# Exponentials of two tiles behind one activation-table load in the expert loop of a fused layer

## The chip, the cores and the metric

The kernel runs on one core of a Trainium2 chip. The metric is the device time of one execution in microseconds (us), here the median of three executions. Five engines work side by side, each through a queue of its own in program order: PE (matrix multiply), ACT (activation functions), DVE and POOL (elementwise work), SP (which here issues nearly all transfers). They meet only through semaphores: an instruction that waits holds up everything behind it on its engine.

## The reference, cut to what matters

One transformer layer over B x T = 4 x 768 = 3072 rows of width 192: retention attention, then a layer of small experts. The change touches only the second part, for each row:

```python
z = jnp.einsum('nd,sdr->nsr', xf, P)                 # S = 8 spaces, R = 16
scores = jnp.einsum('nsr,smr->nsm', z, C)            # M = 64 experts in each space
topv, topi = jax.lax.top_k(scores, K)                # K = 4
w = jax.nn.softmax(topv, axis=-1)
h = jax.nn.gelu(jnp.einsum('nsr,nskrh->nskh', z, W1g) + b1g)
yl = jnp.einsum('nskh,nskhr->nskr', h, W2g) + b2g
comb = jnp.einsum('nskr,nsk->nsr', yl, w)            # then two small dense layers
```

The kernel computes all 64 experts of a space and multiplies each by its gate: the softmax weight if it is among the four largest scores, else 0.

## The kernel before

The rows stand in 24 tiles of 128 (`TILES`) and in 6 blocks of 4 tiles (`NBLK`). After the attention comes the expert loop: 192 groups, `g = 8 i + n`, with 24 iterations `i` of 8 groups `n` each. Four iterations work off one block (block `i // 4`), each group four hidden matrices of 128 x 512. Every engine has this loop written out in its own order.

**One group.** PE: `duo_firsts(g+1)`, `tri_first(g+1)` (L700), `second(g-2)` (L755), `duo_gates(g+1)` (L732), `two_first(g+1)` (L700). ACT: the "duo" gelu (L1051, two banks), the "tri" gelu (L1058), the "two" gelu (L1060). DVE: multiplication of duo by its gates (L1491), of two (L1494). POOL: multiplication of tri by its gates `wbc` (L1686). SP: `spread(g+3)` (L323), which loads the gates `wbc` for three groups ahead and waits until group g-1 is through on DVE and POOL. `second(g)` waits for all three products of its group.

**The gates.** In the same loop the gates of tile `i + 5` (`LEAD`) are made, while `i` is at work. For tile t, in iteration i = t - 5 (some of it at the end of the iteration before): `scores` (PE, L560), `copy_scores` (ACT, L927), `largest` and `mark` (DVE, into `mr`), `distances` (POOL, L1574 and L1576, scores minus the largest, into `dist`), at n = 3 `exps` (ACT, L931), `chosen_exps` and `normaliser` (DVE, L1355 to L1349), `weights` (POOL, L1585), at n = 5 `turn_gates` (PE, L566, transposes into bank `PBANK`), at n = 6 `keep_gates` (ACT, L938), at n = 6 and 7 `high_part` and `low_parts` (POOL, L1592 to L1600, the gates in three bf16 parts in the one buffer `wp`). The results go out to memory: `store_rows` (L275, 2 transfers) at n = 7, and `store_gates` (L282, 3 transfers from `wp`) at n = 0 of the next iteration. They come back once all four tiles of a block are stored: `load_gates(i)` (L305, 3 transfers into `wst`, from which `duo_gates` computes) and `spread`.

Exp and gelu stand in different activation tables, so each `exps` at n = 3 has a table load ahead of it and the next gelu has one too.

Three lines order the transfers. `high_part` overwrites `wp` and so waits, on POOL, until what was stored from it has landed; `load_gates` waits, on SP, for all stores of its block:

```python
                if tile > 0:
                    pool.wait_ge(s["w_stored"], 48 * tile)
...
                sp.wait_ge(s["w_stored"], 48 * min(TILES, 4 * blk + 4))
```

`w_stored` rises by 16 when a transfer has landed, 48 for a tile. `duo_gates(8 i)`, which PE has in group 8 i - 1, waits for `wst_ld`, the landing of `load_gates(i)`.

Of the kernel before, what the change touches and what calls it, by code (L numbers as in the profile page):

```python
# [49 lines left out]
def fused_layer(nc, t):  # L50
# [8 lines left out]
    with ExitStack() as ctx:  # L59
# [39 lines left out]
        with ExitStack() as region:  # L99
            x2 = alloc(region, "x2", [P, 4, D])  # L100
            sc = alloc(region, "sc", [P, S, M + 4])
            mr = alloc(region, "mr", [P, S, M + 4])
# [6 lines left out]
            alloc(region, "spare", [P, 888])  # L109
            x2T = alloc(region, "x2T", [P, 2, BLK])  # L110
            wT_even = alloc(region, "wT_even", [P, 4, BLK])
            dist = alloc(region, "dist", [P, S * M + S * TOPK])
# [105 lines left out]
        def gated(a, b):  # L218

            half = a // HALF  # L220
            return (gate_a, gate_b)[half][:, a - half * HALF:b - half * HALF, :, :]

        def place(g):
# [6 lines left out]
        def _(sp):  # L230
# [131 lines left out]
            for g in range(GROUPS):  # L362
                i, n = divmod(g, 8)
                tile = i + LEAD
                if g + 3 < GROUPS:
                    spread(g + 3)
                if n == 1 and i > 0:
                    load_w2(i, 1)
                if n == 2 and i + 1 < NIT and (i + 1) % 4 != 0:
                    load_gates(i + 1)  # L370
                if n == 4 and i + 1 < NIT and (i + 1) % 4 == 0:
                    load_gates(i + 1)
                if n == 3 and i % 2 == 0 and i + 2 < NIT:
                    load_z(i // 2 + 1)
                if n == 5 and i % 4 == 1 and i > 1:
                    store_out(i // 4 - 1)
                if n == 6 and i in (1, 2, 3):
                    store_z(i + 2)
                if n == 6 and i + 1 < NIT:
                    load_w2(i + 1, 0)  # L380
                if n == 7 and tile < TILES:
                    store_rows(tile)
                if n == 0 and LEAD < tile <= TILES:
                    store_gates(tile - 1)
            store_out(NBLK - 1)
            sp.wait_ge(s["stored"], 16 * 2 * NBLK)
# [3 lines left out]
        def _(pe):  # L390
# [392 lines left out]
            for g in range(GROUPS):  # L783
# [13 lines left out]
                if n == 4 and tile + 1 < TILES:  # L797
                    pe.wait_ge(s["wT_done"], tile)
                    if i > 4:
                        pe.wait_ge(s["fin_h"], 2 * ((i - 1) // 4))  # L800
                    scores(tile + 1, PBANK)
# [30 lines left out]
        def _(act):  # L832
# [96 lines left out]
            def exps(tile):  # L929
                act.wait_ge(s["p_dist"], LENT + tile + 1)  # L930
                act.activation(dist[:, :], dist[:, :], ACT.Exp).then_inc(s["e_done"], 1)  # L931

# [113 lines left out]
            for g in range(GROUPS):  # L1046
# [35 lines left out]
        def _(dve):  # L1082
# [248 lines left out]
            def mark(tile, g0, g1):  # L1331

                if g0 == 0:
                    dve.wait_ge(s["t_top"], tile * 3 + 3)
                    dve.wait_ge(s["p_w"], LENT + tile)
                    carry_waits()
                for g in range(g0, g1):
                    ins = dve.match_replace(mr[:, g, :], top8[:, g, :], sc[:, g, :], TAKEN)  # L1338
                if g1 == S:
                    ins.then_inc(s["t_mr"], 1)  # L1340

            def normaliser(tile):
                dve.wait_ge(s["e_done"], tile + 1)

                dve.wait_ge(s["p_w"], LENT + tile)
                dve.tensor_reduce(norm[:, 0, :], dist[:, S * M:].rearrange("p (s k) -> p s k", k=TOPK), AXX,
                                  ALU.add).then_inc(s["n_done"], 1)
# [3 lines left out]
            def chosen_exps(tile):  # L1351

                dve.wait_ge(s["t_mr"], LENT + tile + 1)
                dve.wait_ge(s["e_done"], tile + 1)
                dve.scalar_tensor_tensor(mr[:, :, 0:M], mr[:, :, 0:M], TAKEN,  # L1355
                                         dist[:, 0:S * M].rearrange("p (s m) -> p s m", m=M),
                                         ALU.is_equal, ALU.mult).then_inc(s["p_em"], 1)
# [126 lines left out]
            for g in range(GROUPS):  # L1484
# [20 lines left out]
                if n in (0, 1) and tile < TILES:  # L1505
# [16 lines left out]
        def _(pool):  # L1522
# [45 lines left out]
            def distances(tile):  # L1568

                pool.wait_ge(s["p_em"], LENT + tile)  # L1570
                pool.wait_ge(s["n_done"], LENT + tile * 2)
                pool.wait_ge(s["t_top"], tile * 3 + 3)
                pool.wait_ge(s["s_copied"], tile + 1)
                pool.tensor_tensor(dist[:, 0:S * M].rearrange("p (s m) -> p s m", m=M), sc[:, :, 0:M],  # L1574
                                   _last(top4[:, :, 0], M), ALU.subtract)
                pool.tensor_tensor(dist[:, S * M:].rearrange("p (s k) -> p s k", k=TOPK), top4[:, :, :],  # L1576
                                   _last(top4[:, :, 0], TOPK), ALU.subtract).then_inc(s["p_dist"], 1)

            def weights(tile):
# [3 lines left out]
                if tile > 0:  # L1583
                    pool.wait_ge(s["t_full"], tile)
                pool.tensor_tensor(wn[:, :, :], mr[:, :, 0:M], _last(norm[:, 1, :], M), ALU.mult).then_inc(s["p_w"], 1)  # L1585

# [93 lines left out]
            for g in range(GROUPS):  # L1680
# [127 lines left out]
```

## Time and profile before

| | |
|---|---|
| median of 3 executions | 987.65 us (986.19 to 988.35) |
| profiled execution, its own time | 985.93 us |
| its span, first to last instruction | 984.1 us |
| PE busy | 897.0 us (91%) |
| DVE busy | 667.6 us (68%) |
| ACT busy | 593.4 us (60%) |
| POOL busy | 477.1 us (48%) |
| table loads on ACT in the whole span | 54, of 1283 ns each |

The expert loop takes the last 57% of the span: its first DVE product starts at 413.5 us. Busy shares are means over stages; what bounds the loop is read from the chain of waits in one iteration.

### The profile page before, as it was taken

To read this page: it belongs to the slowest core of one execution; us is meant where nothing else is said; L and a number is where in the kernel's file an instruction comes from. 1 tells how busy PE (TensorE), PEld (TensorE's weight loads), DVE (VectorE), ACT (ScalarE), POOL (GpSimd) and SP (SyncE) were. 2 spreads that over 40 slices of the span, in tenths; PEclk is the share of its full clock that TensorE was granted. 3 is DMA by queue.
4 is the path that set the end of the run, shared out by engine and by line. 5 is a ranking of instruction groups with operands and counts; after the bars stand their busy time and mean duration, and the time that the engine had idled before them with its cause. 6 is when DMAs were issued, how large, how long until landed. Compare 5 with 4: busy or idle time off the path is not lost.

```text
span 984.1 us, 16064 instructions
## 1 busy us (share of the span) xinstructions
PE 897.0 (91%) x5394; PEld 416.6 (42%) x5394; DVE 667.6 (68%) x1670; ACT 593.4 (60%) x870; POOL 477.1 (48%) x446
## 2 busy tenths in 40 slices
PE   3599999999999967399999999999999999999997
PEld 1267777777677746132222322232232223222322
DVE  4346555666575765277778788788878777777664
ACT  0221211125332343478889898889989888988774
POOL 0133333333343524376656566656665555665443
PEclk8699999999999988589999999999999999999999
DMA  9300001000000029766769797878887978798772
GB/s 264 119 1 1 1 2 69 2 1 1 1 1 20 25 62 122 198 197 203 222 203 271 215 258 231 249 223 243 236 247 234 243 221 243 230 258 264 235 242 94
DMA packets 87110, 151.32 MB, mean 154 GB/s; under 512 B 29984, under 2 KB 54177, under 8 KB 86382
## 3 DMA queue, kind: packets, MB, share of 16 engines
q1 hardware_dynamic: 86158, 147.04, 50.4%
q10 hardware_dynamic: 870, 3.24, 2.7%
q8 instruction: 44, 0.72, 0.3%
q14 instruction: 38, 0.31, 0.1%
HBM read 135.99 MB, written 14.25 MB: 153 GB/s over the span
## 4 chain that ended last, share of the span: by engine, by line
PE 77%; ACT 10%; DVE 6%; issue 5%; POOL 1%; DMA 1%; SPq 0%; ACTq 0%; DVEq 0%; POOLq 0%
PE ps L755 17%; PE ps L700 14%; PE ps L732 8%; PE ps L422 8%; PE ps L430 5%; PE ps L489 3%; PE ps L481 3%; PE ps L498 3%; PE ps L459 2%; ACT ring L1051 2%; PE ps L511 2%; DVE ring L1491 1%; ACT L931 1%; PE ps L566 1%; PE ps L560 1%
## 5 line engine op out<-in xcount | busy, mean ns | idle before, releaser
L1686 POOL TENSOR_TENSOR ring<-ring,wbc 128x512 f32<-128x512 f32 x192 | 245.3, 1282 | 167.5 <-ACT ring L1058 164.7
L1491 DVE TENSOR_TENSOR ring<-ps,ring 128x1024 f32<-128x1024 f32 x192 | 235.1, 1225 | 104.8 <-PE ps L732 73.7
L700 PE MATMUL ps<-zst,w1st 99*128 99x512 bf16 x768 | 213.8, 385 | 15.4 <-ACT ring L1051 13.4
L755 PE MATMUL ps<-ring,w2cur 128*32 128x512 f32 x1536 | 205.6, 608 | 0.0
L1051 ACT ACTIVATE ring<-ps 128x1024 f32<-128x1024 f32 x192 | 197.2, 1027 | 4.2 <-PE ps L700 4.0
L1541 POOL TENSOR_TENSOR t<-t 128x768 f32<-128x768 f32 x48 | 87.4, 1835 | 205.0 <-DVE t L1177 205.0
L1060 ACT ACTIVATE ps<-ps 128x512 f32<-128x512 f32 x192 | 113.8, 593 | 58.4 <-PE ps L700 58.4
L700 PEld LDWEIGHTS ps<-zst,w1st 99*128 99x128 bf16 x768 | 71.9, 98 | 152.2 <-ACT ring L1051 33.6
L1494 DVE TENSOR_TENSOR ring<-ps,wbc 128x512 f32<-128x512 f32 x192 | 130.7, 681 | 0.0
L732 PE MATMUL ps<-wst,sel 96*128 96x512 bf16 x384 | 118.1, 390 | 6.5 <-DVE ring L1491 6.3
L1175 DVE TENSOR_TENSOR t<-ps,rope 128x768 f32<-128x768 f32 x48 | 45.7, 953 | 110.8 <-PE ps L430 74.7
L1058 ACT ACTIVATE ring<-ps 128x512 f32<-128x512 f32 x192 | 115.5, 602 | 0.0
L422 PE MATMUL ps<-wcat,xnT 128*128 128x512 f32 (+1 forms) x240 | 87.0, 502 | 4.9 <-DVE t L1177 4.2
L732 PEld LDWEIGHTS ps<-wst,sel 96*128 96x128 bf16 x384 | 24.7, 98 | 138.1 <-DVE ring L1491 97.1
L851 ACT COPY xnT<-ps 128x384 f32<-128x384 f32 x12 | 5.7, 479 | 122.5 <-PE ps L415 122.5
L755 PEld LDWEIGHTS ps<-ring,w2cur 128*32 128x32 f32 x1536 | 31.7, 108 | 73.3 <-issue 71.6
L422 PEld LDWEIGHTS ps<-wcat,xnT 128*128 128x128 f32 x240 | 43.8, 194 | 36.9 <-issue 26.1
L1585 POOL TENSOR_TENSOR wn<-mr,norm 128x512 f32<-128x512 f32 x24 | 25.1, 1044 | 68.8 <-DVE mr L1355 66.4
L858 ACT COPY qkT<-ps 128x1536 f32<-128x1536 f32 x24 | 34.5, 1438 | 36.0 <-PE ps L481 36.0
L430 PE MATMUL ps<-wcat,xnT 64*128 64x512 f32 (+2 forms) x240 | 48.5, 514 | 0.0
L1338 DVE MATCH_REPLACE8 mr<-top,sc 128x68 f32<-128x68 f32 x192 | 39.0, 214 | 0.0
L481 PE MATMUL ps<-ident,t 128*128 128x128 f32 x288 | 36.0, 275 | 0.8 <-ACT qkT L858 0.8
(166 smaller groups left out, 1144.7 us busy)
## 6 DMA issues: line engine op xcount, KB each, us to landing
wbc<-w_rows SPq DMA_DIRECT2D x192, 512.0 KB, 5.2
w2cur<-in_w SPq DMA_DIRECT2D x48, 256.0 KB, 4.6
w_parts<-wp SPq DMA_DIRECT2D x72, 64.0 KB, 3.3
zst<-z_parts SPq DMA_DIRECT2D x72, 64.0 KB, 5.1
wst<-w_parts SPq DMA_DIRECT2D x72, 64.0 KB, 4.3
w1st<-w_parts ACTq DMA_DIRECT2D x6, 512.0 KB
z_parts<-zp SPq DMA_DIRECT2D x6, 384.0 KB, 5.4
out_h<-h SPq DMA_DIRECT2D x12, 192.0 KB, 4.3
```

The lines of the kernel that those rows point to most:

```text
L422: pe.matmul(bank(to + a // 512, 0, w), xnT[:, k % 2, x, :], wcat[:, 0, col + a:col + a + w], start=True, stop=False)
L430: mm = pe.matmul(bank(to + step * x + a // 512, 0, w), xnT[D2 * x:D2 * x + D2, k % 2, 2, :], wcat[D2 * x:D2 * x + D2, 1, col + a:col + a + ...
L700: return pe.matmul(bank(to), w1st[0:99, 4 * a + j, col:col + P], zst[0:99, (i // 2) % 2, j, :], start=True, stop=True)
L732: mm = pe.matmul(bank(WBANK + j), sel[:, n, :], wst[0:96, i % 2, j, :], start=True, stop=True)
L755: mm = pe.matmul(bank(YBANK, 0, 512, 32 * j, 32 * j + 32), w2cur[:, n, j, :], ring[:, (4 * g + j) % RING, :], start=False, stop=(n == 7 an ...
L1051: act.activation(ring[:, slot:slot + 2, :].rearrange("p a n -> p (a n)"), ps[:, 0:2 * BLK], ACT.Gelu_apprx_tanh).then_inc(s["duo_gelu"], 1)
L1058: act.activation(ring[:, slot + 3, :], bank(TBANK), ACT.Gelu_apprx_tanh).then_inc(s["tri_gelu"], 1)
L1060: act.activation(bank(JBANK), bank(JBANK), ACT.Gelu_apprx_tanh).then_inc(s["two_gelu"], 1)
L1491: dve.tensor_tensor(v, ps[:, WBANK * 512:WBANK * 512 + 1024], v, ALU.mult).then_inc(s["duo_done"], 1)
L1494: dve.tensor_tensor(ring[:, slot + 2, :], bank(JBANK), wbc[:, g % 4, 0, :], ALU.mult).then_inc(s["two_done"], 1)
L1541: pool.tensor_tensor(t1[:, n, :, :].rearrange("p h d -> p (h d)"), t1[:, n, :, :].rearrange("p h d -> p (h d)"), t2[:, n, :, :].rearrange( ...
L1686: pool.tensor_tensor(ring[:, slot, :], ring[:, slot, :], wbc[:, g % 4, 1, :], ALU.mult).then_inc(s["tri_done"], 1)
```

## The change

For tiles 8 to 23 (`paired`) the work goes in pairs of an even tile and the odd one after it. The exponentials of both run at n = 3 of the odd tile's iteration, which is an even `i` from 4 to 18; in the even tile's iteration (odd `i`) there are none. So that two tiles can be under way, `dist` and `mr` have a second buffer each. What follows the exponentials moves too: both tiles' `weights` at n = 3 and 6, `turn_gates` at n = 5 and 7, `keep_gates` at n = 6 and at n = 0 of the next iteration, `high_part` and `low_parts` at n = 0 to 3 of the next iteration, and the stores there as well.

```diff
+        def paired(tile):
+            return tile >= 8
+        def mr_of(tile):
+            return mr_b if paired(tile) and tile % 2 else mr_a[:, :, :]
+        def dist_of(tile):
+            return (dist_b if paired(tile) and tile % 2 else dist_a)[:, :]
+        def before(tile):
+            return tile - 1 if tile > 8 else tile
...
 # sync
-                if n == 4 and i + 1 < NIT and (i + 1) % 4 == 0:
+                if n == 5 and i + 1 < NIT and (i + 1) % 4 == 0:
                     load_gates(i + 1)
...
-                if n == 7 and tile < TILES:
+                if n == 7 and tile < TILES and not paired(tile):
                     store_rows(tile)
-                if n == 0 and LEAD < tile <= TILES:
+                if n == 0 and LEAD < tile <= TILES and not paired(tile - 1):
                     store_gates(tile - 1)
+                if n == 0 and paired(tile - 1) and tile % 2 == 0 and tile <= TILES:
+                    store_rows(tile - 2)
+                if n == 1 and paired(tile - 1) and tile % 2 == 0 and tile <= TILES:
+                    store_rows(tile - 1)
+                if n in (2, 4) and paired(tile - 1) and tile % 2 == 0 and tile <= TILES:
+                    store_gates(tile - 3 + n // 2)
 # tensor
-                    pe.wait_ge(s["wT_done"], tile)
+                    if paired(tile) and tile % 2:
+                        pe.wait_ge(s["wT_done"], tile - 1)
+                        pe.wait_ge(s["s_copied"], tile + 1)
+                    else:
+                        pe.wait_ge(s["wT_done"], tile)
...
-                if n == 5 and tile < TILES:
+                if n == 5 and tile < TILES and not (paired(tile) and tile % 2 == 0):
                     pe.wait_ge(s["s_copied"], min(TILES, tile + 2))
+                    turn_gates(tile - 1 if paired(tile) else tile, PBANK)
+                if n == 7 and tile < TILES and paired(tile) and tile % 2:
+                    pe.wait_ge(s["wT_done"], tile)
                     turn_gates(tile, PBANK)
 # scalar
-                if n == 6 and tile < TILES:
+                if n == 6 and tile < TILES and not paired(tile):
                     keep_gates(tile, PBANK)
+                if n == 6 and tile < TILES and paired(tile) and tile % 2:
+                    keep_gates(tile - 1, PBANK)
+                if n == 0 and paired(tile - 1) and tile % 2 == 0 and tile <= TILES:
+                    keep_gates(tile - 1, PBANK)
...
-                if n == 3 and tile < TILES:
+                if n == 3 and tile < TILES and not paired(tile):
+                    exps(tile)
+                if n == 3 and tile < TILES and paired(tile) and tile % 2:
+                    exps(tile - 1)
                     exps(tile)
 # vector
-                if n == 3 and tile < TILES:
+                if n == 3 and tile < TILES and not paired(tile):
                     chosen_exps(tile)
                     normaliser(tile)
+                if n in (3, 5) and tile < TILES and paired(tile) and tile % 2:
+                    chosen_exps(tile - (n == 3))
+                    normaliser(tile - (n == 3))
 # gpsimd
-                if n == 3 and tile < TILES:
+                if n == 3 and tile < TILES and not paired(tile):
                     weights(tile)
-                if n == 6 and tile < TILES:
+                if n in (3, 6) and tile < TILES and paired(tile) and tile % 2:
+                    weights(tile - (n == 3))
+                if n == 6 and tile < TILES and not paired(tile):
                     high_part(tile)
-                if n == 7 and tile < TILES:
+                if n == 7 and tile < TILES and not paired(tile):
                     low_parts(tile)
+                if n in (0, 2) and paired(tile - 1) and tile % 2 == 0 and tile <= TILES:
+                    high_part(tile - 2 + n // 2)
+                if n in (1, 3) and paired(tile - 1) and tile % 2 == 0 and tile <= TILES:
+                    low_parts(tile - 2 + n // 2)
                 if n == 7 and tile + 1 < TILES:
                     distances(tile + 1)
```

`wp` and `wr` keep one buffer each, and `high_part`, `low_parts`, `load_gates` and `spread` keep their waits.

POOL's instructions in order, before, from the distances of tile 9 (the end of iteration 3) on: products 0 to 6 of iteration 4, the weights at n = 3 and the high part at n = 6. `ring` holds the products, `wn` the weights.

```order
L1574 TENSOR_TENSOR dist<-sc,top 128x512 [waits t_top,s_copied,n_done,p_em]
L1576 TENSOR_TENSOR dist<-top 128x32
L1686 TENSOR_TENSOR ring<-ring,wbc 128x512 [waits spread0,tri_gelu]
L1686 TENSOR_TENSOR ring<-ring,wbc 128x512 [waits spread1,tri_gelu]
L1686 TENSOR_TENSOR ring<-ring,wbc 128x512 [waits spread2,tri_gelu]
L1686 TENSOR_TENSOR ring<-ring,wbc 128x512 [waits spread3,tri_gelu]
L1585 TENSOR_TENSOR wn<-mr,norm 128x512 [waits t_full,n_done,p_em]
L1686 TENSOR_TENSOR ring<-ring,wbc 128x512 [waits spread0,tri_gelu]
L1686 TENSOR_TENSOR ring<-ring,wbc 128x512 [waits spread1,tri_gelu]
L1686 TENSOR_TENSOR ring<-ring,wbc 128x512 [waits spread2,tri_gelu]
L1592 CAST wp<-wT_even 128x256 [waits w_stored,wT_done]
L1594 TENSOR_TENSOR wr<-wT_even,wp 128x256 [waits hi_done]
```

The same engine in the change, from the distances of tile 10 to product 3 of its iteration 5, in which the high and low parts of tiles 8 and 9 are made.

```order
L1617 TENSOR_TENSOR dist_a<-sc,top 128x512 [waits t_top,s_copied,n_done,p_em]
L1619 TENSOR_TENSOR dist_a<-top 128x32
L1729 TENSOR_TENSOR ring<-ring,wbc 128x512 [waits spread0,tri_gelu]
L1635 CAST wp<-wT_even 128x256 [waits w_stored,wT_done]
L1637 TENSOR_TENSOR wr<-wT_even,wp 128x256 [waits hi_done]
L1729 TENSOR_TENSOR ring<-ring,wbc 128x512 [waits spread1,tri_gelu]
L1641 CAST wp<-wr 128x256 [waits r_done]
L1643 TENSOR_TENSOR wp<-wr,wp 128x256 [waits mid_done]
L1729 TENSOR_TENSOR ring<-ring,wbc 128x512 [waits spread2,tri_gelu]
L1635 CAST wp<-wT_even 128x256 [waits w_stored,wT_done]
L1637 TENSOR_TENSOR wr<-wT_even,wp 128x256 [waits hi_done]
L1729 TENSOR_TENSOR ring<-ring,wbc 128x512 [waits spread3,tri_gelu]
```

Both high parts now stand within three products of each other, the second with its wait for `w_stored` ahead of the product of group n = 3; before, eight products lay between two of them.

SP's transfers in order, before, in the last iteration ahead of a new block (the stores of the block's fourth tile, to the load of the next block's first gates).

```order
L323 DMA wbc<-w_rows 128x1x1024 [waits tri_done,two_done,r_stored]
L282 DMA w_parts<-wp 128x2x128 [waits lo_done]
L282 DMA w_parts<-wp 128x2x128 x2
L323 DMA wbc<-w_rows 128x1x1024 [waits tri_done,two_done,r_stored]
L312 DMA w2cur<-in_w 128x512 [waits second_done]
L323 DMA wbc<-w_rows 128x1x1024 [waits tri_done,two_done,r_stored] x3
L305 DMA wst<-w_parts 32x2x512 [waits duo_w,w_stored]
L305 DMA wst<-w_parts 32x2x512 x2
```

And in the change, from the second tile's rows at n = 1 to the same load.

```order
L293 DMA w_rows<-wT_odd 64x2x128 [waits wT_done]
L293 DMA w_rows<-wT_odd 64x2x128
L341 DMA wbc<-w_rows 128x1x1024 [waits tri_done,two_done,r_stored]
L300 DMA w_parts<-wp 128x2x128 [waits lo_done]
L300 DMA w_parts<-wp 128x2x128 x2
L341 DMA wbc<-w_rows 128x1x1024 [waits tri_done,two_done,r_stored] x2
L300 DMA w_parts<-wp 128x2x128 [waits lo_done]
L300 DMA w_parts<-wp 128x2x128 x2
L341 DMA wbc<-w_rows 128x1x1024 [waits tri_done,two_done,r_stored]
L323 DMA wst<-w_parts 32x2x512 [waits duo_w,w_stored]
L323 DMA wst<-w_parts 32x2x512 x2
```

Between the block's last `store_gates` and the `load_gates` that waits for it there were four transfers of `wbc`; now there is one.

## Rows read from the trace of the kernel before

**Rows 1.** The page, busy time, share of the span and instructions of PE

```profile
PE 897.0 (91%) x5394; PEld 416.6 (42%) x5394; DVE 667.6 (68%) x1670; ACT 593.4 (60%) x870; POOL 477.1 (48%) x446
```

**Rows 2.** The chain that ended last, iteration 11, group 3: start us, us, what

```profile
690.77 1.28 ACT L931
692.07 0.55 ACT dist L931
...
694.04 1.03 ACT ring L1051
```

**Rows 3.** Timeline of DVE: duo products of groups in iterations 11, 12, 13, 19

```profile
682.83 1.22 DVE L1491 TENSOR_TENSOR ring<-ps,ring 128x1024 f32<-128x1024 f32 x1
...
690.03 1.23 DVE L1491 TENSOR_TENSOR ring<-ps,ring 128x1024 f32<-128x1024 f32 x1 [0.58 <-PE ps L732]
...
695.09 1.22 DVE L1491 TENSOR_TENSOR ring<-ps,ring 128x1024 f32<-128x1024 f32 x1 [1.24 <-ACT ring L1051]
...
697.63 1.22 DVE L1491 TENSOR_TENSOR ring<-ps,ring 128x1024 f32<-128x1024 f32 x1 [0.72 <-PE ps L732]
...
705.59 1.23 DVE L1491 TENSOR_TENSOR ring<-ps,ring 128x1024 f32<-128x1024 f32 x1
...
728.13 1.23 DVE L1491 TENSOR_TENSOR ring<-ps,ring 128x1024 f32<-128x1024 f32 x1
...
737.93 1.23 DVE L1491 TENSOR_TENSOR ring<-ps,ring 128x1024 f32<-128x1024 f32 x1
...
871.13 1.22 DVE L1491 TENSOR_TENSOR ring<-ps,ring 128x1024 f32<-128x1024 f32 x1 [0.58 <-PE ps L732]
...
890.32 1.23 DVE L1491 TENSOR_TENSOR ring<-ps,ring 128x1024 f32<-128x1024 f32 x1 [0.57 <-PE ps L732]
```

**Rows 4.** The chain that ended last, iteration 12, groups 2 and 3

```profile
712.66 0.99 PE ps L749 x8
...
717.02 0.86 PE ps L560 x2
717.88 0.65 PE ps L700 x3
```

**Rows 5.** Timeline of PE, iterations 11 and 13

```profile
698.33 1.07 PE L755 MATMUL ps<-ring,w2cur 128*32 128x512 f32 x8
...
704.88 0.60 PE L732 MATMUL ps<-wst,sel 96*128 96x512 bf16 x2
...
739.61 0.92 PE L775 MATMUL ps<-g,x2T 65*128 65x192 f32 x4
```

**Rows 6.** Timeline of POOL, end of iteration 11, start of 12

```profile
702.42 0.40 POOL L1592 CAST wp<-wT_even 128x256 bf16<-128x256 f32 x1
...
703.57 1.28 POOL L1686 TENSOR_TENSOR ring<-ring,wbc 128x512 f32<-128x512 f32 x1
704.80 0.39 POOL L1598 CAST wp<-wr 128x256 bf16<-128x256 f32 x1
...
705.90 1.06 POOL L1574 TENSOR_TENSOR dist<-sc,top 128x512 f32<-128x512 f32 x1
...
707.12 1.27 POOL L1686 TENSOR_TENSOR ring<-ring,wbc 128x512 f32<-128x512 f32 x1
```

**Rows 7.** Timeline of SP, iterations 11 and 12: start, issue time, transfers

```profile
687.04 0.35 SPq L312 DMA_DIRECT2D w2cur<-in_w  x1
...
692.52 1.48 SPq L305 DMA_DIRECT2D wst<-w_parts  x3
...
703.13 1.27 SPq L275 DMA_DIRECT2D w_rows<-wT_even  x2
```

**Rows 8.** Line L282 (store_gates), 519 to 872 us

```profile
DMA to landing us min/median/max: 2.4/3.3/4.8
```

**Rows 9.** Line L305 (load_gates), 519 to 872 us

```profile
DMA to landing us min/median/max: 3.5/4.8/7.3
```

**Rows 10.** Line L323 (spread), 519 to 872 us

```profile
DMA to landing us min/median/max: 3.7/5.3/8.5
```

More of the change, by code:

```diff
@@ L100, in fused_layer @@
             x2 = alloc(region, "x2", [P, 4, D])
+            mr_b = x2[:, :, :].rearrange("p a d -> p (a d)")[:, 0:S * (M + 4)].rearrange("p (s m) -> p s m", s=S)
             sc = alloc(region, "sc", [P, S, M + 4])
-            mr = alloc(region, "mr", [P, S, M + 4])
+            mr_a = alloc(region, "mr_a", [P, S, M + 4])
             wr = alloc(region, "wr", [P, 2, P])
@@ L108, in fused_layer @@
             g1b = alloc(region, "g1b", [GH, 8])
-            alloc(region, "spare", [P, 888])
+            dist_b = alloc(region, "dist_b", [P, S * M + S * TOPK])
+            alloc(region, "spare", [P, 344])
             x2T = alloc(region, "x2T", [P, 2, BLK])
             wT_even = alloc(region, "wT_even", [P, 4, BLK])
-            dist = alloc(region, "dist", [P, S * M + S * TOPK])
+            dist_a = alloc(region, "dist_a", [P, S * M + S * TOPK])
             wn = alloc(region, "wn", [P, S, M])
@@ L930, in exps @@
                 act.wait_ge(s["p_dist"], LENT + tile + 1)
-                act.activation(dist[:, :], dist[:, :], ACT.Exp).then_inc(s["e_done"], 1)
+                act.activation(dist_of(tile), dist_of(tile), ACT.Exp).then_inc(s["e_done"], 1)
             def keep_gates(tile, at):
@@ L1334, in mark @@
                     dve.wait_ge(s["t_top"], tile * 3 + 3)
-                    dve.wait_ge(s["p_w"], LENT + tile)
+                    dve.wait_ge(s["p_w"], LENT + before(tile))
+                    if tile == 9:
+                        dve.wait_ge(s["x2_t"], PAIRS)
                     carry_waits()
                 for g in range(g0, g1):
-                    ins = dve.match_replace(mr[:, g, :], top8[:, g, :], sc[:, g, :], TAKEN)
+                    ins = dve.match_replace(mr_of(tile)[:, g, :], top8[:, g, :], sc[:, g, :], TAKEN)
                 if g1 == S:
@@ L1345, in normaliser @@
                 dve.wait_ge(s["p_w"], LENT + tile)
-                dve.tensor_reduce(norm[:, 0, :], dist[:, S * M:].rearrange("p (s k) -> p s k", k=TOPK), AXX,
+                dve.tensor_reduce(norm[:, 0, :], dist_of(tile)[:, S * M:].rearrange("p (s k) -> p s k", k=TOPK), AXX,
                                   ALU.add).then_inc(s["n_done"], 1)
@@ L1354, in chosen_exps @@
                 dve.wait_ge(s["e_done"], tile + 1)
-                dve.scalar_tensor_tensor(mr[:, :, 0:M], mr[:, :, 0:M], TAKEN,
-                                         dist[:, 0:S * M].rearrange("p (s m) -> p s m", m=M),
+                dve.scalar_tensor_tensor(mr_of(tile)[:, :, 0:M], mr_of(tile)[:, :, 0:M], TAKEN,
+                                         dist_of(tile)[:, 0:S * M].rearrange("p (s m) -> p s m", m=M),
                                          ALU.is_equal, ALU.mult).then_inc(s["p_em"], 1)
@@ L1568, in distances @@
             def distances(tile):
-                pool.wait_ge(s["p_em"], LENT + tile)
-                pool.wait_ge(s["n_done"], LENT + tile * 2)
+                pool.wait_ge(s["p_em"], LENT + before(tile))
+                pool.wait_ge(s["n_done"], LENT + before(tile) * 2)
                 pool.wait_ge(s["t_top"], tile * 3 + 3)
                 pool.wait_ge(s["s_copied"], tile + 1)
-                pool.tensor_tensor(dist[:, 0:S * M].rearrange("p (s m) -> p s m", m=M), sc[:, :, 0:M],
+                pool.tensor_tensor(dist_of(tile)[:, 0:S * M].rearrange("p (s m) -> p s m", m=M), sc[:, :, 0:M],
                                    _last(top4[:, :, 0], M), ALU.subtract)
-                pool.tensor_tensor(dist[:, S * M:].rearrange("p (s k) -> p s k", k=TOPK), top4[:, :, :],
+                pool.tensor_tensor(dist_of(tile)[:, S * M:].rearrange("p (s k) -> p s k", k=TOPK), top4[:, :, :],
                                    _last(top4[:, :, 0], TOPK), ALU.subtract).then_inc(s["p_dist"], 1)
@@ L1584, in weights @@
                     pool.wait_ge(s["t_full"], tile)
-                pool.tensor_tensor(wn[:, :, :], mr[:, :, 0:M], _last(norm[:, 1, :], M), ALU.mult).then_inc(s["p_w"], 1)
+                pool.tensor_tensor(wn[:, :, :], mr_of(tile)[:, :, 0:M], _last(norm[:, 1, :], M), ALU.mult).then_inc(s["p_w"], 1)
             def high_part(tile):
```

## The prediction

> **What bounds the kernel now.** I read the busy shares first, then the chain that ended last through the expert loop, then the starts of the duo product on DVE (one for each group), which give every group a length. PE is busy for 91% of the span [rows 1], and the chain confirms it: in a plain stretch it runs from one PE instruction to the next. Iteration 19, which makes no gates, takes 890.32 - 871.13 = 19.19 us for 8 groups, 2.40 us each [rows 3]. That is PE's pace, and whatever adds PE work, or makes PE wait, comes on top.
>
> Iteration 11 (odd i) takes 705.59 - 682.83 = 22.76 us [rows 3]. Its group 3 takes 695.09 - 690.03 = 5.06 where 2.40 is the pace; there the chain leaves PE and goes through ACT: table load, exponentials, table load, gelu [rows 2]. The group after it takes 2.54, and groups 5 to 7 take 705.59 - 697.63 = 7.96, 0.76 more than three plain ones: the gates' transposes and their copy. Iteration 12 (even i) takes 728.13 - 705.59 = 22.54. There the two table loads are in the same place, but the chain runs past them over PE: the extra product with b2 (0.99) and the moved `second` keep PE at work, and the scores (L560) are followed by L700 without a gap [rows 4]. So the loads of odd i are exposed and those of even i are covered. The change takes away the exposed ones.
>
> **What it removes and adds on ACT and PE.** Below, S0 to S8 are the starts of the duo products counted from the start of the iteration.
>
> In 8 odd iterations (3, 5, ... 17) the exponentials and both loads go: 16 loads. Group 3 falls to 2.40. The scores, 0.86 on PE [rows 4], which lay in ACT's stretch, come to light in group 4: 2.54 becomes 3.26. The transposes leave too: 0.76. An iteration falls to 22.76 - 2.66 + 0.72 - 0.76 = 20.06, a gain of 2.70. In iterations 5, 9, 13 and 17 PE has the second half of the final layer in group 3 as well (L775 in [rows 5]); 0.75 of its 0.92 was covered by the loads and comes to light (on PE neighbours overlap: L755 takes 1.07 in the timeline [rows 5] and 0.99 to 1.00 on the chain). There the gain is 1.95. Together 4 x 2.70 + 4 x 1.95 = 18.6 us.
>
> In 8 even iterations there is one more exponential behind the same load: 0.55 on the chain [rows 2]. The cover there is just used up (no gap and no overlap to speak of in [rows 4]), so I take 0.45. Bounds: 0, if the cover is longer than it looks; 0.66, its full length. The second tile's transposes and copy come at n = 7 and 0, at the price of the first: 0.76. On DVE, group 5 gets 1.0 us of `chosen_exps` and `normaliser` beside the maxima; its slack in each later group, the 0.58 of idle time ahead of a product [rows 3], takes most of it, I put 0.1. Sum 1.3 x 8 = 10.5 us given back.
>
> The net of what the change is about is -8.1 us. `mr`, `dist` in two buffers and the waits that follow `before(tile)` only loosen DVE and POOL; they cost nothing, as both have slack. The two waits moved on PE are for events one group or more old.
>
> **What the moved stores cost.** I walk POOL and SP through an odd iteration, first one at a block's end (7, 11, 15, 19), where S = 0, 2.4, 4.8, 7.2, 9.6, 12.9, 15.3, 17.7, 20.06. Durations: a product on POOL 1.28, a high part 1.15 (702.42 to the next product at 703.57), low parts 1.10 (704.80 to 705.90), distances 1.22 (705.90 to 707.12) [rows 6].
>
> - POOL: distances, product 0 until 1.8, high part of the even tile until 3.0, product 1 until 4.25, low parts until 5.35, product 2 until 6.6.
> - SP: rows of the even tile at n = 0; at n = 1 `load_w2` waits for `second` and goes at 4.2 (687.04 - 682.83) [rows 7], then the odd tile's rows (1.27) until 5.85, a `spread` (0.5) until 6.4, then the three stores of `store_gates`, the last issued at 7.3. It lands 3.3 us later at the median, 4.8 at most [rows 8]; I take 4.0, as the third of three comes later than the first. That is 11.3.
> - POOL stands at the second high part from 6.6 until 11.3: `wp` has one buffer. Behind it in the queue is product 3. High part until 12.5, product 3 until 13.8, low parts until 14.9, product 4 until 16.2.
> - PE's `second(3)` comes at S5 + 0.7 (698.33 - 697.63) [rows 3, 5] = 13.6, and waits 0.2 for product 3. SP's `spread(7)` waits for it too (13.9), and lands at 19.2 by the median of 5.3 [rows 10], needed at about S7 + 1.14 = 18.9. So the POOL stall of 4.7 us is nearly swallowed by the two groups of lead.
> - SP: stores of the odd tile after its low parts, the last issued at 15.9, landed at 19.9. Only then does `load_gates`, held on SP, issue its three (1.48 [rows 7]), the last at 20.95; landing takes 3.5 to 7.3, median 4.8 [rows 9], and as little else is under way then I take 4.5: 25.4. `duo_gates(8)` needs it, 0.6 of PE [rows 5] ahead of S8. S8 becomes 26.0 instead of 20.06: **6.0 us of PE idle**. For iteration 19, without scores, it is 26.0 - 19.2 = 6.8.
>
> Sum for four block ends: 3 x 6.0 + 6.8 = 24.8 us. Bounds: with the three landings in series at 3.3, 3.3 and 3.5 it is 3.6 each; at 4.8, 4.8 and 5.4 it is 8.5.
>
> This row can be held against a rule. The trace has landings of 64 KB at 3.3 us median and 2.4 at the least [rows 8]. The Trainium skill, "DMA: Bandwidth & Descriptors", section on the anatomy of one DMA, puts a transfer at about 2.0 us fixed plus its bytes over 436e9, for another issuing path; by it 64 KB would land in an estimated 2.15 us, each of the three landings some 2 us sooner, no block end would stall, and the sum would be -8 instead of the +21 below. The trace does not agree, and it decides.
>
> In the other odd iterations with stores (5, 9, 13, 17), the final layer stretches the first groups (group 0 by 1.86, group 2 by 0.74): S3 = 9.8 (737.93 - 728.13) [rows 3], with S4 = 12.95, S5 = 16.2. No block's gates are waited for, but `load_gates` (1.48) stands ahead of the first stores, and `load_w2` goes 1.85 later. Last store issued at 10.8, landed at 14.8, product 3 done at 17.3, `second(3)` wanted at 16.9: 0.4. `spread(7)` lands at 22.7 for a use at 22.5, `spread(8)`, behind the second stores, at 25.6 for a use at 25.1. I put 1.1 us each, 4.4 in all, between 0 (landings at 3.3) and 3.5 (a `wbc` landing of 7 to 8 us [rows 10]).
>
> **The sum.** -8.1 + 24.8 + 4.4 = +21 us, on the profiled execution's own 985.93: 1007 us. That execution is 1.7 under the median of 987.65, so a median could be 1008 or 1009; I stay at 1007.
>
> **The rivals.**
>
> *Faster: the transfers land soon enough.* If the three landings in series at a block's end take 6 us less in all, `wst` is there when PE wants it; the waits of iterations 5, 9, 13 and 17 go with them, and only the table loads count: -8, 978 us. The point at which it decides is a stall of 2 us a block end (4 x 2 = 8). For it: the transfers at that time have the engines nearly to themselves, as SP stands still. Against it: the least landings are 2.4 and 3.5 [rows 8, 9], which with three of them saves 4.2, not 6. 11 in 100. The Trainium skill's rule cited above would lead here.
>
> *Half the stall.* The stores and loads are quick in the empty stretch (3.0, 3.0, 3.5) and the product waits vanish: some 3 us a block end, +4 to +9, 990 to 996 us. 15 in 100.
>
> *It spreads.* Each late `spread` delays the next by its wait for DVE and POOL, so that an odd iteration loses 3 us where I have 1.1, and each block end 8.5: -8 + 35 + 12 = +39, 1025 us. Landings of 8.5 occur [rows 10], but behind the six transfers of `load_z`, which are not in odd iterations. 9 in 100.
>
> *The loads stay.* If a table load still stood between the two exponentials, the gain would be halved; the built order has 38 loads instead of 54, so this has no chance of its own.
>
> **How the numbers follow.** My forecast, 997 to 1019, has 65 in 100. With half of the second rival the range 994 to 1019 holds about 8 in 10. A measurement of this kernel tells 0.2% (2 us) from no change: slower 0.86 (forecast, half stall, spread), same 0.03 (the lower edge of the half stall), faster 0.11.
>
> **What the profile of the changed kernel would show.** 38 table loads. Odd iterations without block end at some 20 us plus final layer and stall; groups 3 at 2.40. In even iterations group 3 at about 5.7. POOL idle for 4 to 5 us ahead of the second high part, released by the transfer w_parts<-wp. At the ends of iterations 7, 11, 15 and 19 PE idle 5 to 7 us ahead of L732, released by wst<-w_parts, and SP held ahead of `load_gates` for 3 us by w_parts<-wp. If that wait is under 2 us, or not there, the prediction is wrong; if a PE wait for `wbc` comes up in odd iterations, the third rival is at work.

## The result, and the profile after

The changed kernel takes 1011.78 us (median of 4, 1010.48 to 1012.62) against 986.92 us before (median of 4): ratio 1.025, 95% interval 1.0231 to 1.027. It is slower by 25 us. The forecast was 1007, with 994 to 1019 as the range. The profiled execution took 1011.79 us, with a span of 1010.0.

The page of the changed kernel, busy times, and below them its chain that ended last, by engine. They answer to [rows 1].

```profile
PE 902.5 (89%) x5394; PEld 416.8 (41%) x5394; DVE 672.2 (67%) x1670; ACT 573.9 (57%) x854; POOL 475.4 (47%) x446
...
PE 61%; ACT 10%; DMA 9%; DVE 7%; issue 5%; SPq 5%; POOL 3%; ACTq 0%; DVEq 0%; POOLq 0%
```

ACT has 854 instructions, 16 table loads fewer, and is busy for 573.9 us instead of 593.4: the 16 x 1.28 us did go. But 9% of the chain is now transfers and 5% is SP's queue (1% and 0% before). The waits of the loop for transfers, the largest total first (engine, line, waited for: us in total, times, longest), say which.

```profile
POOL wp L1635 <- DMA w_parts<-wp: 47.9, 8, 6.9
...
POOL ring L1729 <- DMA wbc<-w_rows: 26.9, 20, 2.8
...
PEld ps L756 <- DMA wst<-w_parts: 17.8, 4, 5.1
```

Before, the only wait of the loop for a transfer was POOL's for `wbc`, 2.8 us in two places. The first is `high_part` of the odd tile, eight times, 6.0 us each. The third is `duo_gates` at the four block ends; it is the wait of PE's weight loads (PEld), and PE's matmuls stood 14.2 us there in the same four places.

The starts of DVE's duo product through iteration 7 and the first two groups of iteration 8, one line for each group, to be read like [rows 3].

```profile
590.84 1.23 DVE L1531 TENSOR_TENSOR ring<-ps,ring 128x1024 f32<-128x1024 f32 x1
...
593.50 1.23 DVE L1531 TENSOR_TENSOR ring<-ps,ring 128x1024 f32<-128x1024 f32 x1 [0.24 <-PE ps L756]
...
595.90 1.23 DVE L1531 TENSOR_TENSOR ring<-ps,ring 128x1024 f32<-128x1024 f32 x1 [0.18 <-PE ps L756]
...
598.30 1.23 DVE L1531 TENSOR_TENSOR ring<-ps,ring 128x1024 f32<-128x1024 f32 x1 [0.58 <-PE ps L756]
...
600.70 1.22 DVE L1531 TENSOR_TENSOR ring<-ps,ring 128x1024 f32<-128x1024 f32 x1 [0.58 <-PE ps L756]
...
603.96 1.22 DVE L1531 TENSOR_TENSOR ring<-ps,ring 128x1024 f32<-128x1024 f32 x1 [1.44 <-PE ps L756]
...
607.16 1.22 DVE L1531 TENSOR_TENSOR ring<-ps,ring 128x1024 f32<-128x1024 f32 x1 [0.85 <-PE ps L756]
...
610.25 1.22 DVE L1531 TENSOR_TENSOR ring<-ps,ring 128x1024 f32<-128x1024 f32 x1
...
614.95 1.22 DVE L1531 TENSOR_TENSOR ring<-ps,ring 128x1024 f32<-128x1024 f32 x1 [2.27 <-PE ps L756]
...
618.94 1.23 DVE L1531 TENSOR_TENSOR ring<-ps,ring 128x1024 f32<-128x1024 f32 x1 [1.57 <-PE ps L756]
```

Group 3 takes 600.70 - 598.30 = 2.40 (before 5.06), group 4 takes 3.26. Groups 5 and 6 take 3.20 and 3.09, group 7 takes 4.70, and group 0 of the next iteration 3.99, where 2.40 is PE's pace.

SP and then POOL in the same iteration (start, time, instruction, count).

```profile
597.65 2.31 SPq L300 DMA_DIRECT2D w_parts<-wp  x3
600.07 5.84 SPq L341 DMA_DIRECT2D wbc<-w_rows  x2
606.43 1.45 SPq L300 DMA_DIRECT2D w_parts<-wp  x3
...
610.22 1.27 SPq L323 DMA_DIRECT2D wst<-w_parts  x3
```

```profile
596.17 1.28 POOL L1729 TENSOR_TENSOR ring<-ring,wbc 128x512 f32<-128x512 f32 x1
602.93 0.40 POOL L1635 CAST wp<-wT_even 128x256 bf16<-128x256 f32 x1 [5.48 <-DMA w_parts<-wp]
...
604.03 1.27 POOL L1729 TENSOR_TENSOR ring<-ring,wbc 128x512 f32<-128x512 f32 x1
605.25 0.40 POOL L1641 CAST wp<-wr 128x256 bf16<-128x256 f32 x1
```

The even tile's stores go out from 597.65 on. POOL, done with product 2 at 597.45, stands for 5.48 us until they have landed (2.0 us until the third of them is issued, 3.3 us for its landing); product 3 (604.03) and the odd tile's low parts follow, and only after these can SP store (606.43) and, once that has landed, load (610.22). The end of the chain in this stretch (start, length, what):

```profile
607.35 2.86 DMA w_parts<-wp
...
611.07 3.12 DMA wst<-w_parts
...
614.24 0.60 PE ps L756 x2
614.84 1.49 PE ps L724 x4
616.33 1.87 PE ps L779 x8
```

The last two rows are worth a look: 1.49 and 1.87 us for work that takes 0.86 and 1.04 one group later. The windows of the changed kernel (start and end, length, busy us and instructions of PE, PEld, DVE, ACT and POOL; the third number from the end is the granted clock, then the DMA share and GB/s) show why.

```profile
611.00:614.00 3.00, 0.32 (x4) 0.00 (x0) 1.68 (x9) 0.71 (x2) 2.48 (x4) 1.00 0.71 212
615.00:618.00 3.00, 3.00 (x12) 0.36 (x10) 2.36 (x8) 2.10 (x3) 0.47 (x1) 0.50 1.01 364
619.00:622.00 3.00, 2.98 (x18) 0.75 (x15) 2.82 (x7) 2.76 (x5) 0.08 (x1) 1.00 0.42 129
```

After PE had stood nearly idle (0.32 of 3 us), the clock granted was 0.50 (1.2 instead of 2.4 GHz) in the 3 us shown after it had resumed, then 1.00 again. So each block end is paid for twice, the wait and the slow restart.

### The profile page after: what moved, and what is told of

Read it like the earlier page. It is cut to its first block, busy times and chain, and to the rows that moved or that the text cites. A ratio compares the mean times of both kernels' runs of the same rounds, so it can differ in the third digit from the quotient of the medians.

```text
span 1010.0 us, 16049 instructions
## 1 busy us (share of the span) xinstructions
PE 902.5 (89%) x5394; PEld 416.8 (41%) x5394; DVE 672.2 (67%) x1670; ACT 573.9 (57%) x854; POOL 475.4 (47%) x446
## 4 chain that ended last, share of the span: by engine, by line
PE 61%; ACT 10%; DMA 9%; DVE 7%; issue 5%; SPq 5%; POOL 3%; ACTq 0%; DVEq 0%; POOLq 0%
PE ps L779 12%; PE ps L724 9%; PE ps L446 8%; PE ps L756 5%; PE ps L454 5%; DMA w_parts<-wp 4%; PE ps L513 3%; PE ps L505 3%; DMA wbc<-w_rows 2%; PE ps L522 2%; PE ps L483 2%; ACT ring L1082 2%; PE ps L535 2%; DMA wst<-w_parts 2%; SPq L300 1%
## 5 line engine op out<-in xcount | busy, mean ns | idle before, releaser
L779 PE MATMUL ps<-ring,w2cur 128*32 128x512 f32 x1536 | 208.2, 615 | 4.6 <-POOL ring L1729 4.6
L756 PE MATMUL ps<-wst,sel 96*128 96x512 bf16 x384 | 118.5, 391 | 24.2 <-DMA wst<-w_parts 14.2
L756 PEld LDWEIGHTS ps<-wst,sel 96*128 96x128 bf16 x384 | 24.7, 98 | 158.0 <-DVE ring L1531 91.8
L1628 POOL TENSOR_TENSOR wn<-mr_a,norm 128x512 f32<-128x512 f32 x16 | 16.7, 1042 | 43.8 <-DVE mr_a L1395 41.4
L513 PE MATMUL ps<-qkT 128*128 128x128 f32 x288 | 35.0, 278 | 1.4 <-ACT qkT L889 1.1
```

Source lines behind the costliest of these rows:

```text
L756: mm = pe.matmul(bank(WBANK + j), sel[:, n, :], wst[0:96, i % 2, j, :], start=True, stop=True)
L779: mm = pe.matmul(bank(YBANK, 0, 512, 32 * j, 32 * j + 32), w2cur[:, n, j, :], ring[:, (4 * g + j) % RING, :], start=False, stop=(n == 7 an ...
```

## The experiments

**1. A second buffer for the bf16 parts.** The theory: the loss is the wait for landings, and it begins with the one buffer `wp`. After iteration 3 the buffer `zp` is free and holds the odd tiles' parts. Nothing else is changed but the waits that go with it.

```diff
+            wp_b = (zp[:, :, :].rearrange("p k n -> p (k n)")[:, 0:6 * P]
+                    .rearrange("p (k a n) -> p k a n", k=3, a=2))
...
-                    pool.wait_ge(s["w_stored"], 48 * tile)
+                    pool.wait_ge(s["w_stored"], 48 * (tile - 1 if tile > 8 else tile))
+                if tile == 9:
+                    pool.wait_ge(s["st_z"], 16 * NBLK)
```

> The changed kernel with a second buffer for the three bf16 parts (wp): the odd tile's high part no longer waits for the landing of the even tile's stores. Theory one (landings in series: store of the even tile, store of the odd tile, load of the block's first gates, the first held on POOL by the single wp): POOL's 47.9 us of waits for w_parts<-wp vanish, the odd tile's stores go out 4 to 5 us earlier, the PE waits for wst at the four block ends fall from 2.3 to 4.7 us to under 1 us, and with them the spells of halved clock that follow; time 980 to 990 us. Rival (the block end is held by SP's own order of issues or by full DMA engines, not by wp): POOL's waits vanish but the PE waits for wst stay above 2 us each; time 1003 to 1010 us.

Measured 986.96 us, ratio to before 0.9983 (0.9962 to 1.0005). The whole loss is gone, and POOL's wait for `w_parts<-wp` is no longer among the waits. The remaining waits of PE's weight loads for `wst`:

```profile
PEld ps L762 <- DMA wst<-w_parts: 8.2, 4, 2.7
```

8.2 us instead of 17.8. PE's matmuls still stood for it for 3.8 us in three places, 1.8 at most, where I had expected under 1, and one spell of halved clock is left (after iteration 11, from 701.7 us on). So the expectation was missed there, but the time decides against its rival: the one buffer was the cause of the 25 us. But the kernel is only level with the one before, although 8 exposed pairs of table loads are gone. Where that gain went is experiment 5.

**2. Taking the wait for the last stores away.** In the changed kernel, with its one `wp`, the first iteration of blocks 2 to 5 loads the gates of the block before.

```diff
 def load_gates(i):
+                if i % 4 == 0 and blk >= 2:
+                    blk -= 1
                 sp.wait_ge(s["w_stored"], 48 * min(TILES, 4 * blk + 4))
```

> The changed kernel, in which the first iteration of blocks 2 to 5 loads the gates of the block before (long stored) instead of its own, so that nothing waits for the last stores at a block's end; wp keeps its one buffer. The output of those iterations is computed with other gates. Theory one: the wait of PE for wst (14 us in four places) and the spells of halved clock after it (4 x 1.5 us) go, POOL's 47.9 us of waits stay, and so do the longer groups 5 and 6 of odd iterations; time 989 to 996 us. Rival (POOL's waits alone make the loss, through late products and late spreads): time stays above 1004 us.

Measured 1012.73 us, ratio 1.0235 (1.0188 to 1.0282): no better than the change. My theory missed this; the time is as the rival had it, above 1004. The chain in the same place (iteration 7):

```profile
607.42 0.42 SPq L325
...
607.89 5.72 DMA wst<-w_parts
...
613.66 1.03 PE ps L758 x2
```

The iteration starts at 588.64 here and at 590.84 in the changed kernel. So the last transfer is issued 19.3 us after that start instead of 20.2, but takes 5.72 us to land instead of 3.12, right behind the stores and a `wbc` transfer of 512 KB, and lands at 25.0 instead of 23.4. Without the wait for the stores the load is issued little sooner, as SP is held by POOL until then anyway, and lands later.

**3. The same load ahead of everything.** As experiment 2, but the load stands at n = 2 of SP's order, ahead of both stores.

```diff
-                if n == 2 and i + 1 < NIT and (i + 1) % 4 != 0:
+                if n == 2 and i + 1 < NIT and (i + 1) != 4:
                     load_gates(i + 1)
-                if n == 5 and i + 1 < NIT and (i + 1) % 4 == 0:
+                if n == 5 and i + 1 == 4:
```

> As old_gates_at_block_end (one wp buffer; the first iterations of blocks 2 to 5 compute with the gates of the block before), but their load stands at n = 2 of SP's order instead of n = 5, ahead of both stores. Theory (PE's wait at block ends is the time at which SP comes to the load, which one wp buffer delays through POOL, and not the wait for the landing of the last stores alone): the PE waits for wst (17.8 us in the changed kernel) and the spells of halved clock behind them go, POOL's 48 us of waits stay; time 986 to 993 us. Rival (the waits would only pass on to wbc, whose transfers POOL delays as well): time stays above 1000 us.

Measured 1006.65 us, ratio 1.0198 (1.0158 to 1.0239). The wait for `wst` is gone, and other waits stand in its place:

```profile
POOL wp L1637 <- DMA w_parts<-wp: 51.9, 8, 6.8
...
POOL ring L1731 <- DMA wbc<-w_rows: 31.7, 21, 3.8
...
PE ps L781 <- POOL ring L1731: 8.7, 4, 2.7
...
DVE ring L1536 <- DMA wbc<-w_rows: 7.2, 7, 2.7
```

Now PE waits for the late product 3 (L781 is `second`), and DVE for `wbc` whose transfers SP could issue late only. The rival was right here: POOL's standstill delays three things, and `wst` was merely the last of them. The order of landings that I had priced as the loss is one of several paths behind the same 48 us.

**4. Are the loads of odd iterations exposed and those of even ones covered?** Two kernels made from the kernel before, with an identity (which needs no table load) in place of the exponential, once in the even tiles from 8 on (odd iterations), once in the odd ones (even iterations). The lines are the first's; the second has `tile % 2 == 1`.

```diff
-                act.activation(dist[:, :], dist[:, :], ACT.Exp).then_inc(s["e_done"], 1)
+                act.activation(dist[:, :], dist[:, :], ACT.Identity if tile >= 8 and tile % 2 == 0 else ACT.Exp).then_inc(s["e_done"], 1)
```

> The kernel before, with the exponential of the even tiles 8 to 22 replaced by an identity, which needs no table load: the 16 loads of odd iterations go, the activation of dist stays. Those tiles get other gates. Theory one (loads of odd iterations are exposed): group 3 of odd iterations falls from 5.06 to about 2.9 us, the scores come to light in group 4, net about 1.3 to 1.9 us for each of 8 iterations: 10 to 15 us under before, 972 to 977 us. Rival (loads are hidden in either kind of iteration): within 2 us of before.

> The kernel before, with the exponential of the odd tiles 9 to 23 replaced by an identity: the 16 loads of even iterations go. Those tiles get other gates. Theory one (PE's extra work covers them): group 3 of even iterations stays near 5 us or falls by under 0.5 us, time 983 to 987 us. Rival (a load costs its 1.28 us of ACT wherever it stands): 20 us less, 967 us.

Measured 975.18 us (ratio 0.985, 0.9823 to 0.9878) without the 16 loads of odd iterations, and 988.04 us (0.9986, 0.9964 to 1.0009) without those of even ones. The same 20.5 us of ACT time is worth 13 us in one place (by the medians; 15 by the ratio) and nothing in the other. DVE's duo products of groups 3, 4 and 5, first iteration 11 without its loads, then iteration 12 without its:

```profile
685.55 1.22 DVE L1491 TENSOR_TENSOR ring<-ps,ring 128x1024 f32<-128x1024 f32 x1 [0.58 <-PE ps L732]
...
688.22 1.18 DVE L1491 TENSOR_TENSOR ring<-ps,ring 128x1024 f32<-128x1024 f32 x1
...
691.21 1.23 DVE L1491 TENSOR_TENSOR ring<-ps,ring 128x1024 f32<-128x1024 f32 x1 [1.21 <-PE ps L732]
```

```profile
713.48 1.23 DVE L1491 TENSOR_TENSOR ring<-ps,ring 128x1024 f32<-128x1024 f32 x1 [0.17 <-ACT ring L1051]
...
718.00 1.22 DVE L1491 TENSOR_TENSOR ring<-ps,ring 128x1024 f32<-128x1024 f32 x1 [1.77 <-PE ps L732]
...
721.26 1.22 DVE L1491 TENSOR_TENSOR ring<-ps,ring 128x1024 f32<-128x1024 f32 x1 [1.44 <-PE ps L732]
```

Odd: 5.66 us for two groups instead of 7.60 [rows 3]. Even: 721.26 - 713.48 = 7.78, against 5.25 + 2.54 = 7.79 before: the scores come to light in group 4 as the loads leave group 3. So group 3 fell by 0.73, more than the 0.5 that I had expected at most, and group 4 took it all back. The time lies above the 983 to 987 that I expected, but is level with the 988.27 of the kernel before in the same series.

The two times are less clean than these groups. In six iterations from 5 on of the first kernel and seven of the second, the copy of experiment 5 takes 0.70 us instead of 0.18 and group 6 is 0.5 us longer, half of which the next groups give back; and the trace of the kernel before has a spell of halved clock in iteration 15 (24.20 us for 22.76) that neither of the two has.

**5. Where the gain of the two-buffer kernel went.** In it, odd iterations without final layer take 21.5 us (iterations 7 and 15), and I had worked out 20.06. Of the excess, 1.25 is in group 6. DVE there, iteration 7 of the two-buffer kernel:

```profile
604.34 1.16 DVE L1371 COPY top<-top 128x32 f32<-128x32 f32 x1
...
605.62 1.23 DVE L1537 TENSOR_TENSOR ring<-ps,ring 128x1024 f32<-128x1024 f32 x1
```

and POOL beside it:

```profile
604.20 1.27 POOL L1737 TENSOR_TENSOR ring<-ring,wbc 128x512 f32<-128x512 f32 x1 [0.50 <-ACT ring L1099]
```

A copy of 128 x 32 elements takes 1.16 us and ends with POOL's product (605.47). In the kernel before, it took 0.18 us and had started 0.01 us ahead of POOL's L1594 (iteration 11):

```profile
702.89 0.18 DVE L1327 COPY top<-top 128x32 f32<-128x32 f32 x1
702.90 0.71 POOL L1594 TENSOR_TENSOR wr<-wT_even,wp 128x256 f32<-128x256 f32 x1
```

This fits a rule: the Trainium skill, "SBUF — State Buffer", section "SBUF: two separate sides", has the ports that VectorE and GpSimd share as an exclusive lock for a whole instruction, needed by VectorE in a two-port fast mode or with two SBUF inputs (the latter only against a GpSimd instruction that reads SBUF). Two kernels put it to the test, and a third is the control:

```diff
-                dve.tensor_copy(top4[:, :, :], top8[:, :, 0:TOPK])
+                dve.tensor_reduce(top4[:, :, :], top8[:, :, 0:TOPK].rearrange("p s (k o) -> p s k o", o=1), AXX, ALU.max)
# or
+                dve.tensor_tensor(top4[:, :, :], top8[:, :, 0:TOPK], top8[:, :, 0:TOPK], ALU.max)
```

> The kernel with two wp buffers, in which DVE makes top4 from top8 by a reduction over an axis of length one instead of a copy. In the trace of the two-buffer kernel that copy takes 1.16 us instead of 0.18 in odd iterations and ends with the POOL product that runs beside it. Theory one (the copy is shut out while POOL works, and this takes about 1 us off the gain of each odd iteration): the instruction takes 0.18 to 0.2 us everywhere, group 6 of odd iterations falls from 3.65 to 2.7 us, time 978 to 982 us. Rival (the late start of DVE's product has another cause, and the copy merely fills the gap): group 6 stays at 3.65 us and the time within 2 us of the two-buffer kernel's 987.

> The same, but with top4 as the elementwise maximum of top8 with itself, an instruction with two SBUF inputs. If only the fast form of a copy is shut out, it takes some 0.1 us and group 6 falls to 2.7 us, as with the reduction (980 us). If an instruction with two SBUF inputs is shut out by a POOL instruction that reads SBUF as well, it takes up to 1.2 us in odd iterations, and group 6 stays near 3.6 us (985 us).

> The kernel before with the same reduction in place of the copy. There the copy takes 0.18 us in 18 of 19 tiles, since it falls just ahead of a POOL product: theory one says no change, within 1 us of before. Rival (the copy costs in any kernel): 4 us or more faster.

The reduction: 981.36 us, ratio 0.9934 (0.9909 to 0.9958), now clearly under the kernel before. The two-input form: 986.57 us in its one run, level with the copy, and 3.65 us in group 6 of iteration 7 as with the copy. The same line in the trace of the first, then of the second (ns, min/median/max), each with its place in iteration 7 and the POOL instruction beside it:

```profile
L1371 DVE TENSOR_REDUCE top<-top x24: 185/186/189, 281.3 to 838.7; 128x32 f32<-128x32 f32 x24
...
603.46 2.62 POOL L1737 TENSOR_TENSOR ring<-ring,wbc 128x512 f32<-128x512 f32 x2 [2.19 <-DMA wbc<-w_rows]
604.95 0.19 DVE L1371 TENSOR_REDUCE top<-top 128x32 f32<-128x32 f32 x1
```

```profile
L1371 DVE TENSOR_TENSOR top<-top x24: 191/332/1217, 282.4 to 843.6; 128x32 f32<-128x32 f32 x24
...
607.09 1.27 POOL L1737 TENSOR_TENSOR ring<-ring,wbc 128x512 f32<-128x512 f32 x1 [0.35 <-ACT ring L1099]
607.24 1.17 DVE L1371 TENSOR_TENSOR top<-top 128x32 f32<-128x32 f32 x1
```

The reduction, with one input, is shut out in none of its 24 places (189 ns at most), one of them beside POOL's products; the form with two inputs is shut out, as the copy is. That agrees with both halves of the rule, though no trace tells in which mode an instruction ran. In the kernel before, the reduction makes no difference: 986.6 us, ratio 0.9997 (0.9969 to 1.0025). The lockout is not a cost of the copy but of where it falls, and the change moved it: in the kernel before, POOL's `high_part` stood at n = 6 and the copy slipped in just ahead of its second instruction (0.18 us in 15 of the 16 tiles from 8 on); now the product of group 6 is there.

**6. The better version.** Two buffers, the reduction, and the odd tile's parts one group earlier on POOL (n = 1 and 2), its stores at n = 3.

```diff
-                if n in (2, 4) and paired(tile - 1) and tile % 2 == 0 and tile <= TILES:
-                    store_gates(tile - 3 + n // 2)
+                if n in (2, 3) and paired(tile - 1) and tile % 2 == 0 and tile <= TILES:
+                    store_gates(tile - 4 + n)
...
-                if n in (0, 2) and paired(tile - 1) and tile % 2 == 0 and tile <= TILES:
-                    high_part(tile - 2 + n // 2)
-                if n in (1, 3) and paired(tile - 1) and tile % 2 == 0 and tile <= TILES:
-                    low_parts(tile - 2 + n // 2)
+                if n in (1, 2) and paired(tile - 1) and tile % 2 == 0 and tile <= TILES:
+                    low_parts(tile - 3 + n)
+                if n in (0, 1) and paired(tile - 1) and tile % 2 == 0 and tile <= TILES:
+                    high_part(tile - 2 + n)
```

> The two-buffer kernel with the reduction, and with the odd tile's high and low parts one group earlier on POOL (n = 1 and 2 instead of 2 and 3) and its stores at n = 3 instead of 4, so that the block's last stores and the load that waits for them move up by one group. In the two-buffer kernel PE still waited for wst at block ends (0.9 to 1.8 us, and a spell of halved clock once). Theory one: these waits go, 1 to 4 us under wp2_copy_as_reduce, 976 to 980 us. Rival (full DMA engines make the landing late wherever the store stands, 6.4 us for the last store there): no difference.

Measured 979.7 us, ratio 0.9907 (0.9873 to 0.9941), the fastest kernel here that computes all gates, 8 us under the kernel before in the same series. Against the 981.36 of the reduction alone the step is 1.7 us, and the intervals overlap: whether the early parts help is not settled by the times. In the two traces, group 7 of iterations 7, 11 and 15 takes 3.02, 2.35 and 2.35 us instead of 3.59, 2.83 and 2.62, and PE's matmuls wait for `wst` for 0.8 us in one place instead of 2.5 in three.

## Why the prediction was right, and which of its terms were not

**Direction and size.** +21 was forecast, +25 measured by the medians and +26 by the profiled executions (985.93 to 1011.79). The cause was named and is shown by experiment 1: with a second `wp` the loss is gone.

**Exposed and covered loads.** Right, shown by experiment 4 (13 to 15 us, and no difference in time). In the changed kernel group 3 of iteration 7 takes 2.40 and group 4 takes 3.26, both as worked out.

**What the even iterations give back.** Forecast 1.3 us each. In the kernel with the reduction, iterations 6, 10 and 14 take 23.38 us against 22.54 (iterations 6 and 10 before): 0.84. The second exponential costs 0.54 in group 3 (5.79 for 5.25; forecast 0.45). The second transposes and copy were priced at 0.76 and add less there, 0.3 in group 5 and 0.2 in group 7, part of it given back in groups 0 and 1; another 0.27 falls in group 0 of the odd iteration, which I had left out. Why they cost less was not tested.

**The odd iteration's floor.** This term was mis-sized. I had 20.06 us without stalls. The best version shows 20.54 (iterations 11 and 15); the difference is 0.27 each in groups 0 and 6. The two-buffer kernel shows 21.5, another 1.0 for the shut-out copy. "DVE has slack" hid an instruction whose time depends on what POOL does. Over the loop the copy takes 5.6 us (986.96 to 981.36, medians of two series; 4.8 by the ratios to the kernel before) of the -8 that I had as the change's net gain.

**POOL's standstill.** Forecast 4.7 us at a block's end; measured 47.9 in eight places, 6.0 each. It began and ended within 1 us of the walked times (iteration 7: 6.6 to 12.1 after its start, for 6.6 to 11.3). SP was 1.4 us later with the third store than I had walked, and its landing took 3.3 us where I had 4.0.

**The block ends.** Forecast 24.8 us for four. Against a floor of 20.06 (19.19 for iteration 19), iterations 7, 11, 15 and 19 are longer by 4.1, 4.6, 5.7 and 5.9, together 20.3, and the group after each by 1.6, 1.5, 1.5 and 2.1, 6.7 in all, at halved clock. The total of 27 is near, but its parts are not: I had 6.0 us of idle PE ending in the landing of `wst`; beyond the floor there were 2.3 to 4.7 us in group 7, 1.0 to 2.0 in groups 5 and 6 (late products, late `wbc`, and the copy, 0.6 us in iteration 7), and the slow restart, which I had not priced. In iteration 7 `wst` landed 23.4 us after the start, not 25.4: the second store's landing took 2.9 us and the load's 3.1, where I had 4.0 and 4.5. PE's matmuls stood 2.9 to 4.2 us ahead of L756, not the 5 to 7 that I had named as the sign. That the restart makes up for the shorter landings, and so the total comes out near, is luck. And the step "only then does `load_gates` issue", with its wait for the stores as the price, fell in experiments 2 and 3: taking that wait away gives nothing, taking the whole path away gives 5 us, since late products and late `wbc` stand right behind.

**The other odd iterations.** Forecast 1.1 us lost in each of 5, 9, 13 and 17, and a net gain of 0.9. They take 0.5, 0.04, 0.2 and 0.9 us less than before, about 0.4 on average. Both terms were off: the kernel with the reduction, without POOL's standstill, takes 24.2 us in iteration 5 where I had 25.4 - 1.95 = 23.4, a gain of 1.2 and not 1.95; and over that kernel the four lose 0.2 to 1.1 us, 0.7 on average, where I had 1.1. What I did not foresee is that the late `wbc` reaches into the next iteration: iteration 6 takes 26.37 us instead of 22.54. DVE waits there for `wbc` in group 2, and a spell of halved clock follows:

```profile
572.12 0.69 DVE L1534 TENSOR_TENSOR ring<-ps,wbc 128x512 f32<-128x512 f32 x1 [1.46 <-DMA wbc<-w_rows]
```

This is the third rival (it spreads), at one place in eight instead of all. Iterations 14 and 18 show smaller traces of it (0.6 and 1.1 us over the 23.4 of the kernel with the reduction). I read this in the trace alone and did not test it.

## What to carry to other kernels

Work that is put off and paired falls closer together afterwards: count, for each buffer behind a transfer, what used to lie between its two uses. Here eight groups became two, and a landing of 3 us that nobody had waited for, with the issue ahead of it, stopped an in-order engine for 6.

When one engine's standstill delays several others, the wait that comes last carries all the blame in the profile. Removing it alone shows the next one; remove the standstill.

An instruction that got slower without any change to it is read together with its neighbour engine's row: if it ends when that one ends, it may be shut out by it, and another form of the same operation may cure it.

## What the runs showed of the hardware that I had not expected

- A DVE copy of 128 x 32, 0.18 us, took 1.16 us beside a POOL product of 1.27 us that had begun 0.14 us earlier, and a two-input form 1.17 us in the same position; a one-input reduction took 0.19 us in all 24 places.
- Transfers of 64 KB landed in 3.12 us when SP had stood still before them, and in 5.72 us when they were issued right behind other transfers (the last of `load_gates` in iteration 7, changed kernel and experiment 2).
- At all four block ends a wait of PE (2.92, 2.94, 4.18 and 4.16 us) went with half the granted clock, for 3.4 us, beginning 0.3 to 1.2 us after PE's restart, and at the last for 6.8 us, beginning 0.6 us ahead of it, and then full clock again. Shorter waits came ahead of such spells too: 1.55 us in iteration 6 of the changed kernel, 1.72 us in iteration 15 of the kernel before, which is 1.4 us longer than the like iterations, 1.82 us in iteration 11 of the two-buffer kernel. In the kernel with two buffers and the reduction the loop has none from 430 us on to its last microseconds, though PE's matmuls stand there as well, up to 1.8 us (L730).
